# An SSM and expert kernel: own and state products of a chunk moved between its two projections

## The reference

```
xn = layernorm(x)
s  = ssm(xn);  f = experts(xn)
out = x + s * silu(f)
# ssm:
u = silu(causal_conv4(xn @ Wx.T) + conv_b)        # 512 channels, 8 heads of 64
b, c = u @ Wb.T, u @ Wc.T                          # 8 heads x 64 states each
dt = softplus(u @ Wdt.T + b_dt);  a = -exp(log_a)
state = exp(dt*a) * state + (dt*b) outer u         # step by step, per head
y = c . state + d_param * u
s = (norm(y) * silu(xn @ Wz.T)) @ Wout.T           # norm over time, per head
# experts: each of 8 experts takes its best 1024 of 8192 tokens, MLP with silu
```

## Time and profile before

| | us |
|---|---|
| median of three runs | 1216.25 |
| the profiled execution | 1207.71 |
| its span, first to last instruction | 1205.9 |
| TensorE busy | 1181.9 (98%) |
| VectorE busy | 947.5 (79%) |
| GpSimd busy | 774.4 (64%) |
| ScalarE busy | 653.2 (54%) |

### The profile page before, as it was taken

One profiled execution on the slowest core, in us unless ns is written; L12 is line 12 of the kernel. 1 busy time (PEld: TensorE's weight loads), 2 busy tenths in 40 slices (PEclk: granted clock), 3 DMA queues, 4 the chain that ended last, 5 costly groups with the idle time before them and its releaser, 6 DMA issues.

```text
span 1205.9 us, 35027 instructions
## 1 busy us (share of the span) xinstructions
PE 1181.9 (98%) x13979; PEld 973.4 (81%) x13979; DVE 947.5 (79%) x2272; ACT 653.2 (54%) x1406; POOL 774.4 (64%) x726
## 2 busy tenths in 40 slices
PE   9999999999999999999999998999999999999998
PEld 4566668888888878888878787888888888899998
DVE  7999975899987778777778778987767676777676
ACT  5999985454445444444444445455445443545444
POOL 4888945555455667666766658566766645577674
PEclk9999999999999999999999999999999999999999
DMA  9698774544343444443443346555544436799994
GB/s 304 242 360 324 281 277 133 115 154 122 132 148 124 149 126 122 134 144 120 131 140 129 120 126 199 159 151 97 119 92 106 81 80 133 272 333 318 333 333 164
DMA packets 122450, 214.84 MB, mean 178 GB/s; under 512 B 22448, under 2 KB 80560, under 8 KB 117552
## 3 DMA queue, kind: packets, MB, share of 16 engines
q1 hardware_dynamic: 109136, 195.32, 48.1%
q0 software_dynamic: 12288, 17.05, 8.4%
q10 hardware_dynamic: 864, 0.24, 0.1%
HBM read 131.03 MB, written 81.53 MB: 176 GB/s over the span
## 4 chain that ended last, share of the span: by engine, by line
PE 85%; DVE 5%; ACT 2%; DMA 2%; issue 2%; SPq 1%; POOL 1%; ACTq 0%; POOLq 0%; DVEq 0%
PE ps L1406 27%; PE ps L1772 10%; PE ps L2282 8%; PE ps L2261 7%; PE ps L2046 6%; PE ps L1496 3%; PE ps L1418 3%; PE ps L2048 3%; PE ps L1485 3%; PE ps L1473 3%; PE ps L1508 2%; PE ps L1428 2%; PE ps L682 2%; PE ps L630 2%; DMA x_dram<-x 1%
## 5 line engine op out<-in xcount | busy, mean ns | idle before, releaser
L1956 POOL DMA_INDIRECT ffn_dram<-ob,idx x64 | 108.6, 1697 | 83.5 <-DVE ob L1875 68.3
L1356 ACT ACTIVATE decay<-tap,ncum 128x64 f32<-128x64 f32 x344 | 87.0, 335 | 126.7 <-POOL tap L1257 122.3
L1262 POOL TENSOR_TENSOR x_lo<-x,x_hi 128x512 fp32r<-128x512 f32 x56 | 77.3, 1380 | 76.3 <-ACT x_hi L1335 76.3
L1285 POOL TENSOR_SCALAR yb<-x,dcol 128x512 f32<-128x512 f32 x64 | 44.9, 703 | 108.5 <-DMA y_dram<-yb 61.4
L2046 PE MATMUL ps<-dn,mid_hi 128*128 128x512 f32 x288 | 104.8, 399 | 0.5 <-DVE moments L1846 0.5
L2004 ACT ACTIVATE mid<-ps,b_up 128x512 f32<-128x512 f32 x96 | 65.9, 690 | 66.8 <-PE ps L1772 61.4
L1406 PE MATMUL ps<-x_hi,w_hi_b 128*128 128x512 f32 x240 | 99.4, 414 | 0.0
L1406 PE MATMUL ps<-x_hi,w_hi_c 128*128 128x512 f32 x240 | 98.2, 409 | 0.0
L2137 POOL TENSOR_SCALAR yc<-yc,gn_scale,gn_shift 128x512 f32<-128x512 f32 x56 | 77.6, 1397 | 30.9 <-DMA yc<-y_dram 30.9
L1406 PE MATMUL ps<-x_lo,w_hi_b 128*128 128x512 f32 x240 | 94.4, 393 | 0.0
L557 POOL TENSOR_TENSOR acc<-acc,tap 128x512 f32<-128x512 f32 x64 | 82.4, 1291 | 18.0 <-DVE acc L298 13.9
(11 more groups left out here) (327 smaller groups left out, 3853.7 us busy)
## 6 DMA issues: line engine op xcount, KB each, us to landing
x_dram<-x SPq DMA_DIRECT2D x16, 1024.0 KB, 5.6
yc<-y_dram SPq DMA_DIRECT2D x16, 1024.0 KB, 6.7
y_dram<-yb SPq DMA_DIRECT2D x30, 512.0 KB, 3.5
x<-x_dram SPq DMA_DIRECT2D x26, 512.0 KB, 4.8
tap<-cum_half_dram SPq DMA_DIRECT2D x86, 128.0 KB, 3.0
tap<-cum_dram SPq DMA_DIRECT2D x86, 128.0 KB, 3.2
rows_dram<-xn SPq DMA_DIRECT2D x16, 512.0 KB, 3.3
ffn_dram<-zero SPq DMA_DIRECT2D x64, 128.0 KB, 4.1
```

The costliest lines, as they stand in the source:

```text
L1262: nc.gpsimd.tensor_tensor(x_lo[b % 2][:, m, :], x2[b % NX][:, m, :], x_hi[b % 2][:, m, :].bitcast(F32), ALU.subtract).then_inc(x_lo_ready, 1)
L1356: n = nc.scalar.activation(decay[g % 2][:, h, :], key_row[g % NR][:, h, :], ACT.Exp, bias=t.ncum[:, g, h:h + 1])
L1956: pool.indirect_dma_start(out=t.ffn_dram, out_offset=bass.IndirectOffsetOnAxis(ap=t.idx[:, e, h * HC + c:h * HC + c + 1], axis=0), in_=ob[ ...
```

## The change

On TensorE the C projection, with the `turn_b` that belongs behind it where c = 3, goes from in front of the list tiles and the own products to behind the state products; scores and update then follow C. On VectorE the two additions of a chunk's products go from the start of the next chunk to the chunk itself, ahead of the statistics; `mix` goes to the front, then the middle state, then the scaling of x. The computation is the same.

```diff
@@ VectorE, chunk(g)
             first, last = g % SPAN == 0, g % SPAN == SPAN - 1
-            if g:
-                add_state_banks(g - 1)
-            if g:
-                add_other_halves(g - 1)
             if first:
                 clear_y(g)
+            dve.wait_ge(exp_ready, g + 1)
+            dve.wait_ge(s_mm, g + 1)
+            v.tensor_tensor(mix..., ps_scores, decay[g % 2]..., ALU.mult).then_inc(mix_ready, 1)
+            middle_state(g)
             if g == LAST + 1:
                 x.token_lo(dve, 0)
             if g + 1 < NT:
                 scale_x(g + 1)
-            middle_state(g)
-            dve.wait_ge(exp_ready, g + 1)
-            v.tensor_tensor(mix..., ps_scores, decay[g % 2]..., ALU.mult).then_inc(mix_ready, 1)
             if not last:
                 end_state(g)
...
             if LIST0 - 1 <= g < LIST1 - 1:
                 list_slots(g - LIST0 + 1)
+            add_state_banks(g)
+            add_other_halves(g)
             for m in ...: bn_stats
...
         for g in range(NT):
             chunk(g)
-        add_state_banks(NT - 1)
-        add_other_halves(NT - 1)
@@ TensorE
-            if g and b + 1 < NB:
-                project(b + 1, c, 1)
-            if more and c == CH - 1:
-                turn_b(g + 1)
             until(pe, lists_read, listed(g))
             if LIST0 <= g < LIST1:
                 list_tiles(g - LIST0)
...
             state_parts(g, 1).then_inc(y_mm, 1)
+            if g and b + 1 < NB:
+                project(b + 1, c, 1)
+            if more and c == CH - 1:
+                turn_b(g + 1)
             if more:
                 scores(g + 1)
                 update(g + 1)
```

More of the change, by code:

```diff
@@ L1128, in chunk @@
             first, last = g % SPAN == 0, g % SPAN == SPAN - 1
-            if g:
-                add_state_banks(g - 1)
-            if g:
-                add_other_halves(g - 1)
             if first:
                 clear_y(g)
+            dve.wait_ge(exp_ready, g + 1)
+            dve.wait_ge(s_mm, g + 1)
+            v.tensor_tensor(mix.rearrange("p (a h) n -> p a (h n)", a=2), ps_scores,
+                            decay[g % 2].rearrange("p (a h) n -> p a (h n)", a=2), ALU.mult).then_inc(mix_ready, 1)
+            middle_state(g)
             if g == LAST + 1:
@@ L1138, in chunk @@
                 scale_x(g + 1)
-            middle_state(g)
-            dve.wait_ge(exp_ready, g + 1)
-            v.tensor_tensor(mix.rearrange("p (a h) n -> p a (h n)", a=2), ps_scores,
-                            decay[g % 2].rearrange("p (a h) n -> p a (h n)", a=2), ALU.mult).then_inc(mix_ready, 1)
             if not last:
```

## The result

1276.44 us median of four runs (1274.14 to 1278.26) against 1215.34 for the kernel before in the same session: ratio 1.0501, 95% interval 1.0479 to 1.0523, 61.1 us slower. The forecast was +36.6 us, 1253 within 1239 to 1267: the direction was right, the size was not. The profiled execution took 1276.54 us (span 1274.7), 68.8 more than the profiled one of before. That one lay 7.6 us under its kernel's median, so 61.1 of the 68.8 stand in the timed runs.

What follows compares the result with a forecast made beforehand. TensorE, busy 98% of the span, was taken as the bound. Terms 33.6 + 1.1 + 7.0 + 4.0 + 0.4 - 9.5 = +36.6 us put the profiled execution at 1244.3 and the median at 1253 us, range 1239 to 1267.

Steps and rivals of the forecast that it cites:

- The list wait: TensorE's list tiles wait for VectorE's `add_lists` of the same chunk: 24 waits of 1.40 us, 33.6 us slower.
- the eight: Last chunks of blocks in the list stretch, where `add_lists` follows `end_state`: 8 x 0.14 = 1.1 us slower.
- Scores and update come directly behind C. Within a block it costs nothing: Within a block VectorE's mix, middle state, end state and `b_w` are done long before TensorE needs them: no cost.
- the 7.0 forecast: Update waits for `b_w` at block ends: 5.2 us at 12 boundaries plus chunks 7 and 11, together 7.0 us slower.
- the 0.9 at chunks 7 and 11: VectorE late with `b_w` because of its three counts at chunks 7 and 11: 0.9 us each.
- The slot chunks: Chunks 16 to 19: VectorE's slot work behind the additions makes TensorE wait in chunks 18 and 19, 4.0 us slower.
- The ten gaps: TensorE's gaps without a releaser at scores and update, taken as instruction fetches, vanish with C between: -9.5 us.
- The rival in which they stay: The gaps come from something else or move, so 9.5 us are not won: +46, 1262 us; chance 13%.
- The rest: Remaining places: chunk 0 0.4 us; last block 0 within 1 us; no later waits for SyncE's queue.
- Chunk 0: Its x scaling comes behind mix and middle state: between 0 and 0.8 us, taken as 0.4 us slower.
- GpSimd did not become late behind the list wait: Rival: GpSimd's loop to `c_dec` and the state products lengthens, 8 us more, 1261 us; chance 13%.

Runs made afterwards that it cites:

- first experiment: The changed kernel with `add_lists` put ahead of `weigh_b` on VectorE; 1251.13 us, ratio 1.0310 to the kernel before.
- the two runs with repeated transposes: The kernel before with four transposes of B done again in 27 chunks: behind C, 1219.65 us; between state products and scores, 1227.91 us.
- the run of small products made whole again: The changed kernel with `add_lists` ahead of `weigh_b` and, for c < 3, the C projection behind the update; 1258.63 us, ratio 1.0385.
- `weigh_b` first: The changed kernel with `weigh_b` ahead of the slot work in a block's last chunk on VectorE; 1270.71 us, ratio 1.0472.
- the one with both: The changed kernel with `add_lists` ahead of `weigh_b`, `weigh_b` ahead of slot work, and TensorE's and VectorE's old order in the last two blocks; 1240.69 us, ratio 1.0210.

## Why the prediction was wrong

**The list wait** (33.6 forecast) was right in mechanism, place and number: 24 waits, list tiles at T+4.97 (T+5.01 forecast). Its size was 24 x 1.19 = 28.6, since without it the tiles start at T+3.79 (first experiment), not at C's old T+3.61: they are not of C's shape. At the block ends the place was right too, list tiles at T+3.41 for the forecast T+3.4; but where they don't wait (chunk 31) they start at T+3.34, so the eight cost 0.5 us and not 1.1.

**"Scores and update come directly behind C. Within a block it costs nothing"** is the step that failed. It asked only whether operands were ready, and they were. But C between the state products and the scores makes TensorE go from 64x64 to 128x128 products and back once more in each chunk: 0.31 us, in chunks 1 to 57 17.7 us. Nothing in the sum or the range stood for it, and none of the rivals had it. No row of before gives its price, though one hints at half of it: the 32 products of the scores take 0.46 us to the update, the 32 of the update 0.58 to the 128x128 transposes of x. The price took the two runs with repeated transposes. At the block ends 6 to 7 us were lost (15 x 0.4 to 0.5: 9.81 against some 8.9, less 0.31 to 0.35 for the change and 0.07 for the list wait), close to the 7.0 forecast, but mostly at the scores, for ScalarE's `cT`, and not at the update; the 0.9 at chunks 7 and 11 did not come.

**The slot chunks** (4.0) were under-sized. The places were right: chunk 18 at the transposes of B (2.1 us of wait, 1.2 forecast), chunk 19 at the update (2.8, forecast 3.3 of which 0.5 was there). Chunks 16 to 19 lost 6.7 us, and chunk 20 2.1 more by the clock, which no step foresaw; less the change of product size, some 7.

**The ten gaps** (-9.5) went. 23 chunks of 10.45, one of 9.25 and eight of 9.81 make up the list stretch after; the chunks of before without gaps make 285.2 of 295.4, so 10.2 us were gaps, and the run of small products made whole again brought 10.1 us of idle time back. The rival in which they stay fell. The prediction took them for instruction fetches with one packet shown; the kept traces bear it out for all. In the kernel before each of the ten ends 1.1 to 1.5 us after a 16 KiB instruction packet of queue q8 has landed (chunk 39: landed at 552.74, gap from 552.83 to 554.06; chunk 54: landed at 690.69, gap from 691.67 to 692.08). So do the eight gaps of chunks 24 to 55 with C behind the update and the five each in the two kernels with repeated transposes, though such a packet comes only every 7 us. That TensorE is out of instructions in these gaps is still inferred from the times.

**The rest** ("the last block ... 0 within 1 us") missed chunks 58 and 59, 10.4 us: the state products moved from T+7.0 to T+5.2 and T+3.9, under GpSimd's gathers, and behind them the granted clock was 0.50 for 3.4 us in each. Of the tail's 6.0 and of that 10.4 together some 7 belong to the light execution of before. Chunk 0 cost 0.45, forecast 0.4. GpSimd did not become late behind the list wait: `c_dec` cost 1.0 us in the whole loop, forecast 0.

In the timed difference the extra changes (+18), the late chunks (+9) and the slots (+3) stand against a list wait 5 us smaller: within rounding the 24 us between forecast and result.

## What to carry to other kernels

Before moving a block of work, count what it does to TensorE's sequence of product shapes, not only to the waits: a pair of changes between 128x128 and 64x64 products cost 0.31 us here, in each chunk, though every operand was ready. A wait that is predicted right can still be the smaller part of the loss; a chunk timed without its waits, against the old chunk, shows the rest at once. And one profiled execution may be a light one: compare its own time with the median before building small terms on its stages.

## What the runs showed of the hardware

- TensorE's granted clock fell to 0.50, the lower level, during a wait of 2.8 us in chunk 19 and stayed there for 6.8 us; behind the gaps in chunks 58 and 59 it was there for 3.4 us each; the kernel before, with no gap over 1.4 us in its loop, had 1.00 throughout. Taking the wait of chunk 19 away took the stretch away. A wait of 2.1 us in chunk 18 was followed by 3.4 us at 0.50 in three of the kernels (list additions first, `weigh_b` first, and the one with both) and by none in the changed one.
- The gaps without a releaser follow an instruction packet, landed 1.1 to 1.5 us before their end, and came almost only in a long run of small products: but for the 0.3 us at block ends, none in 328 us of lists with C in its middle (one of 0.4 us in the kernel with the old end), 10.1 us in 313 with the run whole. Four transposes in its middle did not end them (3.0 us of idle time, 3.2 with the run whole and the transposes elsewhere).
- GpSimd's indirect gathers held up small products on TensorE in chunks 58 and 59 after the change (state products over 3.5 and 3.1 us in place of 0.65); plain copies of the same size from the same queue did not. No packet of queue q8 is under way in these gaps, so they are not the ones above; and not every overlap with a gather has them.
- VectorE's slot scan took 2.83 us after and 1.55 before. After, GpSimd had a mask from 360.99 to 361.90 and `c_dec` from 361.87 to 363.16 beside it, and the scan ends 1.08 us behind the latter. Before, a mask ended at 352.70 and the scan ends 1.06 us behind that; `c_dec`, begun during the scan, was the one that took longer, 1.92 us in place of 1.29. The Trainium skill (SBUF — State Buffer, section SBUF: two separate sides) says that a VectorE operation with two SBUF inputs and GpSimd share a pair of ports by an exclusive lock; these rows agree.

Before:

```profile
352.21 1.55 DVE L998 TENSOR_TENSOR_SCAN spare<-cst,chosen 128x512 f32<-128x512 f32 x1
```

After:

```profile
361.41 2.83 DVE L998 TENSOR_TENSOR_SCAN spare<-cst,chosen 128x512 f32<-128x512 f32 x1
```
